# Epsilon and the means' negation as two-tensor operations, and GpSimd's state remainder between the second and third scatter

## What is computed

```
g = sigmoid(LN(x) @ Wg.T + bg);  h[t] = (1 - g[t]) * h[t-1] + g[t] * LN(x)[t]   # along a sequence
x = x + LN(h @ Wo.T + bo)                                                        # LN: no scale, no shift
xf = LN(x); eid = argmax(xf @ router_w + router_b)       # one of 8 experts
rank = tokens of the same expert before this one; valid = rank < 320
y = relu(xf @ w1[eid] + b1[eid]) @ w2[eid] + b2[eid] if valid else relu(xf @ ow1 + ob1) @ ow2 + ob2
x = x + LN(y)
```

## Time and profile before

| | |
|---|---|
| median of 3 runs | 1178.93 us (1178.27 to 1179.01) |
| the profiled execution | 1179.15 us, of which 1177.3 us span |
| busy share of the span | PE 96%, PEld (weight load) 84%, DVE 89%, ACT 65%, POOL 55% |
| granted TensorE clock | 0.998 of full speed |

### The profile page before, as it was taken

One profiled execution on the slowest core, in us unless ns is written; L12 is line 12 of the kernel. 1 busy time (PEld: TensorE's weight loads), 2 busy tenths in 40 slices (PEclk: granted clock), 3 DMA queues, 4 the chain that ended last, 5 costly groups with the idle time before them and its releaser, 6 DMA issues.

```text
span 1177.3 us, 24621 instructions
## 1 busy us (share of the span) xinstructions
PE 1131.3 (96%) x7341; PEld 991.5 (84%) x7341; DVE 1044.9 (89%) x2793; ACT 767.5 (65%) x1433; POOL 647.7 (55%) x734
## 2 busy tenths in 40 slices
PE   8999999999999999999999999999999999999996
PEld 4788888888888888888888888888888888899996
DVE  6888899999999999999999999999999988778885
ACT  4366666666667666666666666766766667678783
POOL 3556656665555655555666555565555555414544
PEclk9999999999999999999999999999999999999999
DMA  8211132222222222222222222222222130245440
GB/s 252 65 45 63 33 107 78 68 66 55 71 71 71 71 71 68 66 68 58 61 65 60 54 71 71 71 71 71 69 66 68 50 104 19 80 146 181 147 132 34
DMA packets 186314, 92.46 MB, mean 79 GB/s; under 512 B 121403, under 2 KB 182509, under 8 KB 186148
## 3 DMA queue, kind: packets, MB, share of 16 engines
q1 hardware_dynamic: 179108, 86.65, 26.5%
q0 software_dynamic: 7168, 5.34, 1.5%
HBM read 53.82 MB, written 38.76 MB: 79 GB/s over the span
## 4 chain that ended last, share of the span: by engine, by line
DVE 46%; PE 32%; issue 16%; ACT 2%; POOL 2%; DVEq 1%; DMA 0%; ACTq 0%; POOLq 0%
DVE st L940 11%; DVE hid_lo L1104 5%; PE psY L1528 5%; PE psY L1531 4%; PE psY L1530 4%; PE psH L1420 4%; PE psH L1421 4%; PE psH L1422 4%; DVE mv L947 3%; DVE psT L983 3%; DVE ysb L1118 3%; DVE outt L1034 2%; DVE att L1011 2%; DVE xfT_lo L1048 2%; DVE hst L1005 2%
## 5 line engine op out<-in xcount | busy, mean ns | idle before, releaser
L1528 PE MATMUL psY<-W_hi,hid_hi 128*128 128x256 f32 x1168 | 339.6, 291 | 27.2 <-DVE hid_lo L1104 27.1
L1531 PE MATMUL psY<-W_hi,hid_lo 128*128 128x256 f32 x1168 | 330.2, 283 | 0.0
L1530 PE MATMUL psY<-W_lo,hid_hi 128*128 128x256 f32 x1168 | 330.0, 283 | 0.0
L686 ACT ACTIVATE hid<-psH,biasT 128x512 f32<-128x512 f32 (+1 forms) x312 | 201.7, 647 | 154.9 <-PE psH L1422 153.4
L1528 PEld LDWEIGHTS psY<-W_hi,hid_hi 128*128 128x128 f32 x1168 | 222.4, 190 | 52.3 <-DVE hid_lo L1104 39.6
L453 POOL TENSOR_TENSOR rstd<-veps,mhalf 128x4 f32<-128x4 f32 (+2 forms) x103 | 124.1, 1205 | 203.9 <-DVE nmean L952 203.9
L1420 PE MATMUL psH<-xfT_hi,W_hi 128*128 128x512 f32 (+1 forms) x624 | 235.9, 378 | 0.3 <-ACT hid L686 0.2
L1421 PE MATMUL psH<-xfT_lo,W_hi 128*128 128x512 f32 (+1 forms) x624 | 234.9, 376 | 0.0
L1422 PE MATMUL psH<-xfT_hi,W_lo 128*128 128x512 f32 (+1 forms) x624 | 232.7, 373 | 0.0
L1530 PEld LDWEIGHTS psY<-W_lo,hid_hi 128*128 128x128 f32 x1168 | 222.9, 191 | 3.4
L1531 PEld LDWEIGHTS psY<-W_hi,hid_lo 128*128 128x128 f32 x1168 | 222.8, 191 | 0.0
(11 more groups left out here) (177 smaller groups left out, 2213.8 us busy)
## 6 DMA issues: line engine op xcount, KB each, us to landing
xin<-L_attn_x SPq DMA_DIRECT2D x32, 512.0 KB, 3.5
stage<-L_ffn_w SPq DMA_DIRECT2D x16, 1024.0 KB, 5.7
out<-outt SPq DMA_DIRECT2D x31, 512.0 KB, 2.8
stage<-L_attn_x SPq DMA_DIRECT2D x26, 512.0 KB, 3.4
stage<-tok SPq DMA_DIRECT2D x416, 32.0 KB
xbuf<-zrow SPq DMA_DIRECT2D x1, 2590.0 KB, 17.1
xin<-xbuf SPq DMA_DIRECT2D x8, 259.0 KB, 5.2
stage<-L_ffn_ow SPq DMA_DIRECT2D x2, 1024.0 KB, 9.2
```

Of the source, the lines that this page charges most:

```text
L686: act.activation(hid[j % 2][:, at:n], psH[:, j % 2, at:n], ACT.Relu, bias=bias).then_inc(s_hid, 1)
L1528: pe.matmul(dst, hi, w[0][:, j, :], start=(j == 0 and (tail or t % 2 == 0)), stop=False, skip_group_check=True)
L1530: pe.matmul(dst, hi, w[1][:, j, :], start=False, stop=False, skip_group_check=True)
L1531: last = pe.matmul(dst, lo_, w[0][:, j, :], start=False, stop=(j == HC - 1), skip_group_check=True)
```

## The change

`moments` adds epsilon and negates the mean with two-tensor operations against constant tiles, which two added memsets fill at the start, and waits for them by one more semaphore. In `step` (used from the third group on) POOL's `state_lo(far)` is issued between the second and the third scatter of `now`, where it stood behind the fourth. `dispatch` is called twice for this, so its waits and its `sem_inc` are issued twice too.

```diff
+        eps_t = sb("eps_t", [P, TG])
+        minus = sb("minus", [P, TG])
...
+        s_eps = sem("s_eps")
...
@@ gpsimd, step
                 if live(now, NG):
-                    dispatch(now, range(TG))
+                    dispatch(now, range(0, 2))
                 if live(far, NG):
                     state_lo(far)
+                if live(now, NG):
+                    dispatch(now, range(2, TG))
@@ vector, start
+            dve.memset(eps_t[:], EPS)
+            dve.memset(minus[:], -1.0).then_inc(s_eps, 1)
@@ vector, moments
-                dve.tensor_scalar(veps[k][:, t0:n].unsqueeze(2), mv[k][:, t0:n, 1:2], EPS, None, ALU.add)
-                dve.tensor_scalar(nmean[k][:, t0:n].unsqueeze(2), mv[k][:, t0:n, 0:1], -1.0, None, ALU.mult)\
+                dve.wait_ge(s_eps, 1)
+                dve.tensor_tensor(veps[k][:, t0:n].unsqueeze(2), mv[k][:, t0:n, 1:2], eps_t[:, t0:n].unsqueeze(2), ALU.add)
+                dve.tensor_tensor(nmean[k][:, t0:n].unsqueeze(2), mv[k][:, t0:n, 0:1], minus[:, t0:n].unsqueeze(2), ALU.mult)\
                     .then_inc(s_ve[k], 1)
```

## The result

The changed kernel takes 1140.68 us (median of 4 runs, 1139.86 to 1141.23), against 1178.92 for the kernel before on the same chip. The ratio is 0.9676, 95% interval 0.9659 to 0.9693: 38.2 us faster. The profiled execution has a span of 1138.3 us, 39.0 less than before, at a granted clock of 0.997.

A forecast was written before the change was run, and what follows sets the result against it. PE has nearly all the work, but DVE, held once a step by POOL's state_lo, sets its pace. PE's waits before L1528 (30.6 us) and Rank waits (3.0) taken from 1179.15 gave 1145.6, forecast 1145.4; range 1141 to 1159.

The forecast's parts named there:

- T: Zero point of a step's times: the start on PE of the eight transposes of tok2.
- B: At L951 DVE waits through one scatter as well, is only about 0.95 us earlier: 1155 us; chance 0.14.
- C: At L951 DVE waits through both scatters behind the moved state_lo; each step 0.45 us longer: 1190 us; chance 0.10.
- the small operation that waited only 0.16 us: A 128x32 DVE operation beside POOL's L468, four in a row: 0.35 us against 0.19, cited against C.
- A: All of PE's waits before L1528 and before the rank matmuls go: 1145.4 us, own range 1142 to 1150; chance 0.68.
- the sum: PE's waits before L1528 and Rank waits together: 33.6 us, or 1.34 a step, all taken as saved.
- PE's waits before L1528: PE's waits for hid_lo, once a step: 26.6 us by the view plus 25 x 0.16 for modelled ends, 30.6.
- Rank waits: PE's small second wait before the rank matmuls in odd steps: 11 x 0.27 = 3.0 us.
- odd steps: Steps where PE lost 1.31 us before layer2(3) and 0.27 before the rank matmuls; even ones lost 1.14 only.
- my terms of 1.58 and 1.14: PE's predicted loss per step to DVE's lateness: 1.58 us in an odd step, 1.14 in an even one.
- The slack: After the change hid_lo(3) would end 0.6 us before PE wants it, in both even and odd steps.

The follow-up runs named there:

- the padding: Extra bn_stats on DVE (0.33 us each) added to the changed kernel: four ahead of hid_lo(3), 1158.37 us; seven between norm 0's nmean and ysb, 1185.38 us.

## Why the prediction was wrong in size and right in kind

- **What bounds the kernel** was right: DVE's wait for POOL, paid by PE once a step. Delaying DVE alone at that place brings PE's waits back (26.9 us against 26.6), with POOL's order as changed.
- **The move** was right in its times: `state_lo` T+2.33 to T+4.88 (forecast 2.3 to 4.9), `nmean` at T+4.82 (4.9), the scatters' end T+7.30 (7.5), POOL's remaining wait 1.25 us (1.1).
- **The two-tensor form** costs nothing and brings nothing. It waits for 0.4 us, as I took it, but so does the one-source form once `state_lo` is moved, and in the old order both wait for the whole of `state_lo`. The Trainium skill, "SBUF — State Buffer", section "Who interferes with whom", was right that the two-tensor form contends all the same (2.62 us with the forms alone).
- **Rivals.** B and C did not happen, in either form: `veps` ended before the third scatter began, 0.15 us after `state_lo`. My reason against C, the small operation that waited only 0.16 us, did not carry over, since in the old order the two-tensor form waited for both halves. C's premise (DVE does not get in between POOL's instructions) was true of `state_lo`'s two halves and of the memset, and not of L468. What let DVE in behind the moved `state_lo` is not shown: it may be POOL's pause of 0.15 us, or that a scatter doesn't hold DVE at all, as `hid_lo` beside one suggests. No run takes the pause away or puts a pause without a scatter between the halves. So A came true without the reason that I gave against C, and that much of it was luck.
- **What failed is the sum**, "PE's waits before L1528 ... 30.6. Rank waits ... 3.0 ... Together 33.6 us". It holds only the waits that I had found with a mark or looked for. The start times give 63.71 - 60.57 = 3.14 us a pair of steps, 39.2 us over 25, against 33.6. It left out 0.1 us at the matmul behind each large wait (also seen when a wait was made with the padding) and the odd steps' wait of 0.14 + 0.08 at `layer2(0)`. The trace of before had two signs of it. The odd step was 32.18 us and the even one 31.52, 0.66 apart, where my terms of 1.58 and 1.14 give 0.44. And the weight loads of L1528 waited 33 times in the window where PE has 25 marked waits. The range of case A, which allowed 3 us for small gaps that I couldn't see, ended at 1142 for the same reason, and the whole one at 1141.0, 0.3 us too high.
- **The slack** of 0.6 us at `hid_lo(3)` was nearly right for odd steps (0.54) and too small for even ones (1.0). It did not matter for the time, since both are above zero.

## What to carry to other kernels

When an engine's tiny operation has a median of 0.17 us and a maximum of 2.8, look at what its neighbour does in that time, and move the neighbour's work by a few instructions before changing the form of the small one: here the move was worth 39 us and the forms nothing. Size a gain not by adding marked waits but by the period of the loop: the starts of the same instruction two steps apart, less what the bounding engine needs when it runs without a gap. Read the slack in each kind of step, since an odd and an even one differed by 0.5 us and the smaller one set the price.

## What the runs showed of the hardware

A DVE instruction that has to wait for POOL can wait longer than the POOL instruction under way: both forms of `veps` stood through the two halves of `state_lo` back to back (2.57 and 2.62 us against 1.3 for one), and through those two with a memset between them (2.81 and 2.83 us). It doesn't always: behind a one-source L468 that was followed at once by another, DVE's two-input operations waited for the one alone (0.35 us in all at 131.40, 1.36 at 140.99), and in the second case the next L468 took 1.53 us in place of 0.55. The Trainium skill, "SBUF — State Buffer", "Who interferes with whom", has the loser blocked for the other's whole instruction. The L468 cases agree with that; at `state_lo` the measurement is longer than one instruction, and it decides. What makes the difference between the two is open: the number of POOL's inputs, the length of the instruction (0.55 against 1.3 us) and the kind of DVE's operation all differ.

PE lost 0.1 us more at the matmul after each large wait: 0.22 us from the first to the second 256-column matmul, where 0.11 or 0.12 is the pace. Behind the odd step's small wait of 0.14 it was 0.20. The same 0.20 stands behind the rank matmuls in both kernels (611.00 to 611.20 before, 649.22 to 649.42 now), with a wait ahead of them or without, so it isn't a mark of waits alone.
